# Exponentials, low parts and normalised rows shared out block by block between VectorE, ScalarE and GpSimd

## What is computed

```python
x = x + xattn0(layernorm(x), ctx, mask)    # 16 heads of 32, no output projection, masked keys at -inf
x = x + ffn0(layernorm(x))                 # rows quantised to 8 bits, ternary weights unpacked from int32
x = x + xattn1(layernorm(x), ctx)          # 16 heads of 64, then an output projection
x = x + ffn1(layernorm(x))                 # real(ifft(fft(x) @ w_freq)) + bias: a linear map of each row
```

## Time and profile before

| | us |
|---|---|
| median of 3 runs | 1040.56 (1039.41 to 1041.71) |
| profiled execution, its own time | 1040.61 |
| span in the profile | 1037.5 |
| busy: PE, DVE | 897.2 (86%), 835.0 (80%) |
| busy: ACT, POOL | 648.9 (63%), 579.0 (56%) |
| mean granted clock of PE | 0.967 |

### The profile page before, as it was taken

The page is one execution under the profiler, slowest core; times in us unless marked ns, Lnnn a source line. Parts: engine busy times, 40 slices in busy tenths (PEclk is TensorE's granted clock), DMA queues, the critical chain, the costliest instruction groups (busy, mean ns, idle before and its releaser), DMA issues.

```text
span 1037.5 us, 17964 instructions
## 1 busy us (share of the span) xinstructions
PE 897.2 (86%) x6236; PEld 495.0 (48%) x6236; DVE 835.0 (80%) x1451; ACT 648.9 (63%) x1808; POOL 579.0 (56%) x588
## 2 busy tenths in 40 slices
PE   0799798978679988998899899989999998799587
PEld 0447574544335544554445445545554454444343
DVE  7997869799887898789978997899788968845724
ACT  2538853676865696669666966796578746525710
POOL 3306664543654678467747774776478636715513
PEclk9999999988889999999999999999999999899989
DMA  8871669594757566847593858485857554622605
GB/s 290 144 174 29 129 137 158 159 226 94 139 85 150 83 127 109 196 74 134 104 201 68 151 99 194 80 146 100 186 95 132 106 132 82 123 41 65 115 8 162
DMA packets 352904, 130.39 MB, mean 126 GB/s; under 512 B 333487, under 2 KB 342640, under 8 KB 349999
## 3 DMA queue, kind: packets, MB, share of 16 engines
q1 hardware_dynamic: 352815, 129.25, 61.0%
HBM read 33.57 MB, written 15.96 MB: 48 GB/s over the span
## 4 chain that ended last, share of the span: by engine, by line
PE 36%; DVE 27%; ACT 11%; POOL 10%; DMA 7%; issue 6%; SPq 3%; ACTq 0%; DVEq 0%; POOLq 0%
PE wb L264 10%; PE wb L265 10%; PE wb L266 10%; ACT pr L1039 5%; DMA prT<-ph 4%; POOL pr L885 3%; DVE xh L1320 3%; PE wb L1581 3%; DVE ph L1402 3%; DVE parts L1117 2%; ACT xh L1064 2%; DVE mx L1382 2%; DVE xr L1336 2%; POOL xr L911 2%; POOL xn L900 2%
## 5 line engine op out<-in xcount | busy, mean ns | idle before, releaser
L885 POOL TENSOR_TENSOR pr<-pr,sm 128x616 f32<-128x616 f32 x128 | 177.8, 1389 | 225.9 <-DVE sm L1397 225.9
L1039 ACT ACTIVATE pr<-scores,bound,factor 128x77 f32<-128x77 f32 x576 | 230.5, 420 | 8.5 <-POOL ph L890 2.1
L264 PE MATMUL wb<-xT,wq_hl 128*128 128x512 f16 (+1 forms) x400 | 151.5, 379 | 15.5 <-DMA xT<-xh 8.2
L265 PE MATMUL wb<-xT,wq_hl 128*128 128x512 f16 (+1 forms) x400 | 151.4, 378 | 0.0
L266 PE MATMUL wb<-xT,wq_hl 128*128 128x512 f16 (+1 forms) x400 | 151.2, 378 | 0.0
L1052 ACT ACTIVATE ph<-pr 128x618 f16<-128x618 f32 x128 | 93.5, 731 | 46.6 <-POOL pr L885 33.2
L1039 ACT ACTIVATION_READ_ACCUMULATOR pr<-scores,bound,factor 128x1 f32 x576 | 119.5, 207 | 0.0
L264 PE MATMUL wb<-wo_hl,qc 128*128 128x512 f16 x276 | 105.6, 383 | 5.5 <-DVE x L1336 3.2
L266 PE MATMUL wb<-wo_hl,qc 128*128 128x512 f16 x276 | 105.6, 383 | 0.0
L265 PE MATMUL wb<-wo_hl,qc 128*128 128x512 f16 x276 | 105.6, 383 | 0.0
L1320 DVE TENSOR_TENSOR xh<-xn,xh 128x1024 f16<-128x1024 f32 x48 | 76.9, 1601 | 22.7 <-ACT xn L1067 9.4
(11 more groups left out here) (232 smaller groups left out, 2443.0 us busy)
## 6 DMA issues: line engine op xcount, KB each, us to landing
xr<-in_x SPq DMA_DIRECT2D x6, 1024.0 KB, 5.9
out_x<-xr SPq DMA_DIRECT2D x5, 1024.0 KB, 5.1
xr<-in_wk SPq DMA_DIRECT2D x3, 1024.0 KB, 6.9
xr<-in_wq SPq DMA_DIRECT2D x3, 1024.0 KB, 10.2
xr<-in_wv SPq DMA_DIRECT2D x3, 1024.0 KB, 5.7
k1b<-scr_k SPq DMA_DIRECT2D x16, 154.0 KB, 4.3
...
```

The lines of the kernel that those rows point to most:

```text
L264: pe.matmul(out, lhs(0), rhs(0), start=start, stop=False, **kw)
L265: pe.matmul(out, lhs(0), rhs(1), start=False, stop=False, **kw)
L885: pool.tensor_tensor(v, v, s, ALU.mult).then_inc(probs_ready, 1)
L1039: ins = act.activation(pr[U % 3][:, h // 4, cols], sc[:, U % 2, h // 4, cols], ACT.Exp, bias=bound[:, U % 2, h:h + 1], scale=k["factor"][: ...
```

## The change

The three rules become functions of the unit *and its block* (`headwise`, `low_by_pool`, `rows_by_pool`), a general set with exceptions for single blocks. By the general set the low parts of X4, X5 and X6 go from POOL to DVE and the rows of (2, 2) to ACT. With the exceptions, POOL has 1, 4, 4, 2, 2, 4, 5 and 6 low parts of X units in blocks 0 to 7, where it had five in each: eight low parts go to DVE in blocks 2 to 6, three of them in block 3 and three in block 4. Over the whole program 68 units are headwise (72 before), 46 low parts are POOL's (56) and 26 pairs of rows (32).

The slot tables change with it: FILLS in eight of 18 slots (Z f 2 one slot later, Z out 1 and 2 in slot 6 between X pv 0 and 1), APPLY and LOWER for j = 1 a slot later, and all the tables of the head and of the tail. Some weights are split in other slots, half a weight gets a semaphore of its own (`wk1_second`, `wv1_second`), and loads and stores stand at other places of SP's list.

```diff
 FILLS
-FILLS = [[("Z", "f", 0), ("Z", "f", 1), ("Z", "f", 2)],
-         [("Z", "f", 3)],
+FILLS = [[("Z", "f", 0), ("Z", "f", 1)],
+         [("Z", "f", 2), ("Z", "f", 3)],
...
-         [("Z", "out", 1)],
-         [("X", "pv", 0), ("X", "pv", 1)],
          [],
-         [("Z", "out", 2), ("Z", "out", 3), ("Y", "q", 0), ("Y", "q", 1), ("Y", "q", 2), ("X", "pv", 2), ("Y", "q", 3)],
+         [("X", "pv", 0), ("Z", "out", 1), ("X", "pv", 1), ("Z", "out", 2)],
+         [],
+         [("Z", "out", 3), ("Y", "q", 0), ("Y", "q", 1), ("X", "pv", 2), ("Y", "q", 2), ("Y", "q", 3)],
...
-ROWS_BY_POOL = {(2, 0), (2, 2), (3, 0), (3, 2)}
-LOW_BY_POOL = {("X", 1), ("X", 4), ("X", 5), ("X", 6), ("X", 7), ("Y", 0), ("Y", 1)}
+ROWS_BY_POOL = {(2, 0), (3, 0), (3, 2)}
+LOW_BY_POOL = {("X", 1), ("X", 7), ("Y", 0), ("Y", 1)}
+OWN_HEADWISE = {("X", 0, 0), ("X", 1, 0), ("X", 1, 5), ("X", 1, 7), ("X", 2, 0), ("X", 4, 1), ("X", 5, 7), ("X", 6, 7),
+                ("X", 7, 5), ("X", 7, 7), ("Y", 1, 7), ("Y", 2, 6), ("Y", 3, 6), ("Y", 3, 7)}
+OWN_LOW_BY_POOL = {("X", 0, 1), ("X", 0, 2), ("X", 1, 0), ("X", 1, 1), ("X", 1, 5), ("X", 2, 7), ("X", 3, 1), ("X", 3, 2),
+                   ("X", 3, 5), ("X", 3, 6), ("X", 3, 7), ("X", 4, 0), ("X", 4, 5), ("X", 4, 6), ("X", 4, 7), ("X", 5, 1),
+                   ("X", 5, 2), ("X", 5, 5), ("X", 6, 6), ("X", 6, 7), ("X", 7, 0), ("X", 7, 2), ("Y", 0, 7), ("Y", 1, 6),
+                   ("Y", 1, 7), ("Y", 2, 0), ("Y", 2, 7), ("Y", 5, 0), ("Y", 5, 1), ("Y", 5, 5)}
+OWN_ROWS_BY_POOL = {(0, 0, 1), (0, 0, 2), (0, 0, 5), (0, 0, 6), (2, 0, 2), (2, 2, 0), (2, 2, 7), (3, 0, 5), (3, 0, 7),
+                    (3, 2, 5)}
+def headwise(v):
+    return (v[:2] in HEADWISE) != (v in OWN_HEADWISE)
...
-BIAS = {9: [(3, 0), (1, 0)], 15: [(1, 2)], 16: [(2, 2)], 17: [(3, 2), (2, 0)]}
+BIAS = {9: [(1, 0)], 10: [(3, 0)], 15: [(1, 2)], 16: [(2, 2)], 17: [(3, 2), (2, 0)]}
...
-                if (i, s) == (1, 12):
+                if (i, s) == (1, 15):
                     split_high("WO", 0)
-                if (i, s) == (2, 1):
+                if (i, s) == (2, 2):
                     split_high("WO", 1)
...
-                if (i, s) == (1, 14):
+                if (i, s) == (1, 10):
                     load_v(1, 0)
```

More of the change, by code:

```diff
@@ L536, in probs_lo @@
         def probs_lo(n):
-            by_pool = unit_numbered(n)[:2] in LOW_BY_POOL
-            return lo_by_pool if by_pool else lo_by_dve, sum(1 for v in UNIT if UNIT[v] <= n and (v[:2] in LOW_BY_POOL) == by_pool)
+            by_pool = low_by_pool(unit_numbered(n))
+            return lo_by_pool if by_pool else lo_by_dve, sum(1 for v in UNIT if UNIT[v] <= n and low_by_pool(v) == by_pool)
         def unit_at(g):
@@ L1030, in exp @@
                 f = F_E0 if stage == "X" else F_E1
-                if (stage, u) in HEADWISE:
+                if headwise((stage, u, b)):
                     n = F_N0 if stage == "X" else F_N1
@@ L1035, in exp @@
                         act.wait_ge(*probs_lo(U - 3))
-                    act.wait_ge(bounded, sum(1 for v in UNIT if UNIT[v] <= U and v[:2] in HEADWISE))
+                    act.wait_ge(bounded, sum(1 for v in UNIT if UNIT[v] <= U and headwise(v)))
                     for h in range(8):
@@ L1065, in ln_apply @@
                                              bias=shift[:, j, t:t + 1], scale=rstd[:, j, t:t + 1])
-                    if (j, pair) not in ROWS_BY_DVE and (j, pair) not in ROWS_BY_POOL:
+                    if (j, pair) not in ROWS_BY_DVE and not rows_by_pool((j, pair, b)):
                         ins = act.activation(xn[:, t - pair, :], xs(b)[:, t, :], ACT.Identity,
@@ L1392, in sums @@
                 dve.wait_ge(exp_done, U + 1)
-                if (stage, u) not in HEADWISE:
+                if not headwise((stage, u, b)):
                     step(dve.tensor_reduce(sm[:, U % 4, :].rearrange("p (g h) -> p g h", g=2), four(pr[U % 3][:, :, 0:GK]), AX.X, ALU.add))
-                if (stage, u) in LOW_BY_POOL:
+                if low_by_pool((stage, u, b)):
                     step(dve.tensor_scalar(sm[:, U % 4, :], sm[:, U % 4, :], 1.0 / PS, None, ALU.mult))
@@ L1411, in _ @@
             first_maxima()
-            ln0(0)
             scaling("WK0")
             split_low("CTX")
-            maximum("WQ0", wq0_in)
+            ln0(0)
+            split_low("WK0")
+            maximum("WV0", wv0_in)
             for g, (i, s) in enumerate(SLOTS):
                 if (i, s) == (-1, 0):
-                    maximum("WV0", wv0_in)
                     with_bias("WV0", 1, vb0[0:1, :])
-                    split_low("WK0")
-                if (i, s) == (-1, 2):
                     maximum("WF", wf_in, 0, 8)
+                if (i, s) == (-1, 3):
+                    maximum("WQ0", wq0_in)
@@ L1487, in _ @@
                     sums(*unit_at(g - 1))
-                if unit_at(g - 2) and unit_at(g - 2)[:2] not in LOW_BY_POOL:
+                if unit_at(g - 2) and not low_by_pool(unit_at(g - 2)):
                     probs_low(*unit_at(g - 2))
```

162 lines of the change are left out of this document (84 added, 78 removed), and 115 rows, old and new, of tables (OWN_APPLY, OWN_BIAS, OWN_FILLS, OWN_LOWER).

## The result

| | before | changed kernel |
|---|---|---|
| median of 16 runs each | 1039.5 us (1034.74 to 1041.71) | 1042.6 us (1040.4 to 1049.57) |
| ratio to before, 95% interval | | 1.0041 (1.0028 to 1.0055) |
| profiled execution / span | 1040.61 / 1037.5 us | 1045.27 / 1043.5 us |
| busy PE, DVE | 897.2, 835.0 | 901.2, 847.9 |
| PE idle (span minus busy) | 140.3 | 142.3 |

It leaves out runs in a slower state, of which there was one, of 1052.4 us among the twelve of sp_order.

A forecast was written before the change was run, and what follows sets the result against it. No one engine bounds everywhere: in steady blocks DVE, then PE; head and tail hold more idle time. Head -6.7, steady -1, tail -3, -8 and -0.5 sum to -19.2: 1040.6 to 1021.4 us, range 1008 to 1034.

The forecast's parts named there:

- Step (2): Set-up: reordered DVE work and changed kinds of units in block 0 cancel out; 0 us, between -2 and +3.
- Step (1): Head, block 0: X5's low part on DVE removes PE's 5.15 us transpose wait; -2.5 us, between 0 and -5.15.
- Step (3): Head, block 0: q 4 and q 5 partly fill PE's 5.07 us wait ahead of Y0's scores; -1 us.
- Step (4): Head: WO's high part on ACT, three slots later, shortens PE's 5.92 us wait for exponentials; -1.2 us.
- Step (5): Head: v1b's six loads issued earlier on SP shorten PE's 3.07 us transpose wait; -2 us, between 0 and -3.07.
- Steady blocks: Five middle blocks: low parts moved to DVE fit its idle time; -1 us for all five, between -3 and +8.
- Steps (6) and (7): Tail: direct units and moved fills shorten PE's waits for exponentials and transposes; block 6 -3 us, block 7 -8 us.
- the case: Whole kernel, the forecast itself: 1021.4 us, 1014 to 1028 with head, steady and tail ranges; chance 0.56.
- (8): Tail: stores of blocks 5 and 6 are issued before the last fills; -0.5 us.
- DVE in the X stage: Rival, behind slot 6 in six blocks: PE waits for DVE's drains, 4 us a block, total 1045 us; chance 0.09.

The follow-up runs named there:

- sp_order: The changed kernel with the second of SP's two set-up row transposes moved behind the stores of keys; ratio to before 0.9964 (0.9941 to 0.9987).
- before_early: The kernel before with both first pairs of rows transposed earlier on SP, in set-up slot 5 instead of 8; ratio 1.0022 (1.0002 to 1.0043).
- only_steady: The kernel before with the change's steady blocks alone (iterations 2 to 6); ratio 0.9996 (0.9980 to 1.0012).
- only_tail: The kernel before with the change's tail alone (iterations 7 to 11); ratio 1.0001 (0.9986 to 1.0016).
- y13_direct: The kernel before with only units Y1 and Y3 of block 7 made direct instead of headwise; ratio 1.0001 (0.9985 to 1.0016).

## Why the prediction was wrong, step by step

**Step (2), set-up: it failed, and with the wrong sign it decides the result.** I gave it 0, between -2 and +3. It is +7.8 us in the trace and +0.6% alone. I had gone through what moved on DVE, and not through SP: two DMA transposes were moved ahead of stores that were ready, and one of them waits for a product of DVE. "What is queued behind the waiting instruction" was the question, and the answer was stores, at their end those whose landing ACT needs. A hint was in the trace of before, where SP spent 9.4 us on the two transposes from 45.99; what held it there was another thing (see before_early).

**Step (1), X5 of block 0.** The mechanism was right (no wait for `prT` between 120 and 130 us), the size was not: of 5 us, discounted to 2.5, nothing is left at block 2. I asked for the next late thing only at the weight chain, 97 us on. It was 1 us on: DVE's low parts of the keys of layer 1 and of a product, 2.54 and 1.84 us.

**Step (3)** had the wait right: 5.07 became 2.85. It doesn't show at the end. **Step (4)** failed: the 5.92 us don't depend on WO's high part at all. I had seen it ahead of the wait in ACT's list and taken that for a cause; the one-edit run leaves the wait unchanged. **Step (5)**: the wait went; what it gave is between 0 and the 2 us forecast, and its size stays open.

**Steady blocks** were right, -1 forecast, -0.4 (0.9980 to 1.0012 as a ratio) measured, with a cost inside that I had not thought of (last section). That the low parts pay for standing beside POOL was a side matter: DVE's, now 82, take 1029 ns in the mean, 1040 before; POOL's multiplications went from 1389 to 1439 ns (1419 in only_steady), 6 us more in 128, of an engine that is idle for nearly half the time. By the Trainium skill ("SBUF — State Buffer", section "SBUF: two separate sides") the one who comes second waits out an instruction. The trace agrees on POOL's side, with those 50 ns in the mean; on DVE's side the mean shows nothing of it.

**Steps (6) and (7), tail: -11.5 forecast, +0.1 us measured** (only_tail, 0.9986 to 1.0016). This was the largest term. Two errors. First, one engine's gain was counted without the other's price in the same chain: in y13_direct ACT's 5.2 us came back as DVE's 4.12 us wait. Second, fills laid into a gap come from elsewhere. In only_tail PE's waits from Y0 to Y7 of block 7 fell from 7.5 to 2.8 us, and those between Y7 of block 6 and Y0 of block 7 rose from 2.1 to 7.0 (2.17 and 3.16 the longest), after the last Y unit from 7.7 to 10.0. The sum from block 7's first unit to the end was 28.1 us before and 29.9 in that run. I had subtracted waits and never asked that their sum should fall, which it only does if a chain gets shorter.

**The sum.** With SP's order mended the change is worth 0.4%, some 3.7 us, of 19.2; that would be some 1036 us, and still outside the range. So the sign comes from step (2), and the size of the miss mostly from the tail. Six of the terms, (1) and (3) to (7), were of the form "this wait goes", and all six had the same bias: none asked on every engine what was late next. A slip of adding lies in the range of the case too: head -3, steady +2, tail -7 and (8) give 1032, not 1028. The chance of 0.09 for slower was for another place (DVE in the X stage), and no rival had the set-up at more than +3.
